# Attention inside a fused block: the products for the row maxima ahead of the weighing in TensorE's order

## The reference, cut to what matters

```python
qkv = x @ W_qkv                      # 16 heads of 64
q, k = apply_rope(q), apply_rope(k)
dots = jnp.einsum('bhid,bhjd->bhij', q, k) * scale
dots = jnp.where(causal, neg, dots)
attn = jax.nn.softmax(dots, axis=-1)
out = jnp.einsum('bhij,bhjd->bhid', attn, v)
out = jax.nn.relu(out @ W_o1) @ W_o2
```

## Time and profile before

| | us |
|---|---|
| median of three runs (5065.14 to 5069.31) | 5067.33 |
| the profiled execution | 5057.61 |
| its span, first to last instruction | 5056.0 |
| VectorE busy | 3705.1 (73%) |
| TensorE busy (matmuls) | 3693.8 (73%) |
| ScalarE busy | 2569.0 (51%) |
| POOL busy | 2388.5 (47%) |
| largest group: L2242, `low_part`, 640 times | 783.7 |
| next: L2269, `maximum`, 748 times | 667.0 |

### The profile page before, as it was taken

The page is one execution under the profiler, slowest core; times in us unless marked ns, Lnnn a source line. Parts: engine busy times, 40 slices in busy tenths (PEclk is TensorE's granted clock), DMA queues, the critical chain, the costliest instruction groups (busy, mean ns, idle before and its releaser), DMA issues. The chain is left out here.

```text
span 5056.0 us, 84627 instructions
## 1 busy us (share of the span) xinstructions
PE 3693.8 (73%) x28905; PEld 2609.3 (52%) x28907; DVE 3705.1 (73%) x4463; ACT 2569.0 (51%) x4134; POOL 2388.5 (47%) x1532
## 2 busy tenths in 40 slices
PE   2997645555555569948936898989989899894595
PEld 1663224444444446637813566666656566663484
DVE  6883489999999988840067888888888888885101
ACT  1222456666666632222313677777767676684221
POOL 0220268888888842221034665655656666600202
PEclk9998777777676779959957999999999999996697
DMA  2000001000000100024532222222222222202255
GB/s 86 0 0 4 7 21 32 30 29 29 29 31 30 30 29 0 0 91 146 175 113 58 57 51 52 48 47 68 53 64 54 50 54 52 55 10 92 73 182 155
DMA packets 236313, 276.22 MB, mean 55 GB/s; under 512 B 63820, under 2 KB 183557, under 8 KB 234561
## 3 DMA queue, kind: packets, MB, share of 16 engines
q1 hardware_dynamic: 223056, 244.85, 17.7%
q0 software_dynamic: 8704, 24.35, 1.4%
q10 hardware_dynamic: 4224, 2.76, 0.3%
HBM read 152.60 MB, written 36.04 MB: 37 GB/s over the span
## 5 line engine op out<-in xcount | busy, mean ns | idle before, releaser
L2242 DVE TENSOR_TENSOR att_b_prob_low<-att_b_prob,att_b_prob_high 128x1024 f16<-128x1024 f32 (+2 forms) x640 | 783.7, 1225 | 54.5 <-ACT att_b_prob_high L2209 49.0
L2269 DVE TENSOR_REDUCE att_b_neg_max<-att_b_peek 128x1 f32<-128x1024 f32 (+1 forms) x748 | 667.0, 905 | 143.3 <-PE att_b_peek L2097 114.0
L2207 ACT ACTIVATE att_b_prob<-att_b_score,att_soft 128x1024 f32<-128x1024 f32 (+2 forms) x640 | 633.0, 989 | 223.7 <-PE att_b_score L2120 148.0
L1025 PE MATMUL mix_scan_hT<-ident,mix_scan_h 128*128 128x128 f32 x1024 | 253.3, 395 | 526.6 <-DVE mix_scan_h L973 498.6
L2209 ACT ACTIVATE att_b_prob_high<-att_b_score,att_soft 128x1024 f16<-128x1024 f32 (+2 forms) x640 | 630.1, 985 | 10.2 <-PE att_b_o L2148 3.5
L1025 PEld LDWEIGHTS mix_scan_hT<-ident,mix_scan_h 128*128 128x128 f32 x1024 | 176.5, 200 | 640.7 <-DVE mix_scan_h L973 445.1
L2144 PE MATMUL att_b_o<-att_b_vh,att_b_prob_high 128*128 128x65 f16 x4352 | 463.1, 195 | 37.2 <-DVE att_b_prob_low L2242 26.5
L2118 PE MATMUL att_b_score<-att_b_q_both,att_b_k_twice 128*128 128x512 f16 (+3 forms) x1280 | 448.9, 351 | 28.6 <-ACT att_b_prob_high L2209 18.3
L2144 PEld LDWEIGHTS att_b_o<-att_b_vh,att_b_prob_high 128*128 128x128 f16 x4352 | 401.4, 98 | 130.4 <-DVE att_b_prob_low L2242 71.5
L2148 PE MATMUL att_b_o<-att_b_vh,att_b_prob_low 128*128 128x65 f16 x4352 | 461.8, 194 | 0.0
L2146 PE MATMUL att_b_o<-att_b_vl,att_b_prob_high 128*128 128x64 f16 x4352 | 461.4, 193 | 0.0
(11 more groups left out here) (343 smaller groups left out, 9606.0 us busy)
## 6 DMA issues: line engine op xcount, KB each, us to landing
moe_w<-in_L_ffn_W_dram SPq DMA_DIRECT2D x64, 1024.0 KB, 8.2
mix_scan_b_row<-mix_b_rows SPq DMA_DIRECT2D x128, 256.0 KB, 3.1
att_b_crossed<-att_b_raw SPq DMA_DIRECT2D x512, 64.0 KB, 2.0
att_b_q_both<-att_b_halves SPq DMA_DIRECT2D x240, 64.0 KB, 2.0
att_b_k_twice<-att_b_halves SPq DMA_DIRECT2D x240, 64.0 KB, 2.0
moe_slots_in<-moe_route_zero SPq DMA_DIRECT2D x2, 4096.0 KB, 14.3
moe_exp_x<-moe_slots_in SPq DMA_DIRECT2D x32, 256.0 KB, 4.5
moe_slots_out<-moe_exp_y POOLq DMA_DIRECT2D x32, 256.0 KB, 6.4
```

What stands on the lines that cost most here:

```text
L1025: last = pe.transpose(hT_ps[:, j * D + m * P:j * D + (m + 1) * P], hs[:, b * W + m * GRP + t * P:b * W + m * GRP + (t + 1) * P], ident[:, :])
L2207: act.activation(prob[:, at:at + width], score[m % 2][:, 0:width], ACT.Exp, scale=soft[:, 0:1])
L2242: dve.tensor_tensor(prob_low[:, at:at + width], prob[:, at:at + width], prob_high[:, at:at + width], ALU.subtract).then_inc(low_ready, 1)
L2269: last = dve.tensor_reduce(neg_max[:, first + col:first + col + 1], peek_bank(kind, s)[:, base:base + nb * P], AX.X, ALU.max, negate=True)
```

## The change

In TensorE's order within a step `peek` stands in front of `weigh` instead of behind it. The orders of the other engines and all semaphore counts are as before, and so are all operations.

```diff
                     if has_piece(kind, v):
                         scores(t, b, v, kind)
-                    if v >= 2 and has_piece(kind, v - 2) or v < 2 and has_piece(kind, -1):
-                        weigh(t, b, v - 2)
                     peek_at = slot_at(kind, v)
                     if peek_at:
                         peek(t, b, kind, *peek_at)
+                    if v >= 2 and has_piece(kind, v - 2) or v < 2 and has_piece(kind, -1):
+                        weigh(t, b, v - 2)
                     job = side_job(kind, v)
                     if job:
                         side(t, b, *job)
```

## The result

The kernel got **0.8% slower**: 5105.29 us median of four runs (5102.17 to 5109.34) against 5066.24 (5061.6 to 5069.31) of the kernel before, ratio 1.0082, 95% interval 1.0071 to 1.0094. That is +39 us where +55 was forecast, inside the range and with the forecast's sign. The profiled execution took 5102.17 us, its span 5100.6: 44.6 us more than the profiled execution before, whose time lay 9.7 us under its median of three.

What follows compares the result with a forecast made beforehand. Attention keeps VectorE 86% and TensorE 89% busy; POOL sets steps 1 to 21, later steps lack cover. Terms 2.66 + 0.63 + 0.39 = 3.68 us a pair, times 15, give 55 us slower: 5122 us, range 5062 to 5187.

Steps and rivals of the forecast that it cites:

- the last pair: The pair of heads with no successor to prepare; the forecast multiplied its loss by the 15 other pairs only.
- Steps 23 to 39: Second part of a pair, without cover from POOL: late maxima delay TensorE, 2.66 us a pair.
- the four terms: Late maxima at steps 24, 26, 28, 34: 1.36, 1.61, 0.59, 1.43 us, less 2.33 us of waits already there.
- a wait taken at the latest step serves its neighbours: Steps 23 to 39: TensorE then stands later against VectorE, so only the peaks of lateness were counted.
- Step 22: The weighing, formerly ahead of the wait for keys, now runs behind it with all that follows: 0.63 us a pair.
- Step 0: Late maximum delays the next pair's first projection, so POOL's unbroken run starts later: 0.39 us a pair.
- Steps 1 to 21: Costed at nothing: small losses end in a shorter wait for keys, 5.41 us, at step 22.
- Set by POOL: Steps 1 to 21: POOL's rotations run without a break until the keys step 22 needs, and set the time.
- Faster: Rival: early products feed a starving VectorE; at most 54 us of the maxima's idle time goes, 5013 us; chance 0.12.
- no change: Rival: TensorE takes its waits at other places and VectorE loses 6 us, 5073 us, within 0.2%; chance 0.12.
- The ring: Rival: maximum, products, weighing, exponential, subtraction release each other, 4.92 us per two steps, nearly everywhere; 5187 us; chance 0.12.
- The clock: Rival: more waits bring more falls of TensorE's clock, 6 us on top of the forecast, 5128 us; chance 0.04.

Runs made afterwards that it cites:

- the first two experiments: New order only in steps 23 to 39, then only in steps 0 to 22, against the kernel before: ratios 1.0081 and 1.0002.
- the fourth experiment: Changed kernel with the old order again at steps 24, 26, 28 and 34: 5104.43 us, ratio 1.0050 to the kernel before.
- short maxima: Each row maximum over half its columns: 5079.98 us (1.0024) with the new order, 5015.08 us (0.9900) with the old, ratios to the kernel before.
- the fifth experiment: Changed kernel with four halves of `prob_high` in place of two: 5116.12 us, ratio 1.0103 to the kernel before.
- M first: New order only in steps 23 to 39, with VectorE's maximum ahead of the low-half subtraction from step 24: 5116.35 us, 1.0083 to the kernel before.
- the kernel with both edits: Kernel before with the new order in steps 1 to 21 and step 22's products for the maxima behind the values job: 5041.89 us, 0.9943.
- The two gains: Against the kernel before: new order only in steps 0 to 21, 0.9967; old order with step 22's products behind the values job, 0.9968.

## Why the prediction was right, and where it was not

The number came out in part by luck: the mechanism of the largest term held, one term was sized too high, and two places put at nothing, the run on POOL and the last pair, erred in opposite directions.

**Steps 23 to 39: 2.66 us predicted, 2.98 measured.** The mechanism, K behind a late M with W and the scores queued behind it, is shown by the first two experiments and by K's idle time (28.5 to 152.6 us). The sizes of the four terms were good in sum (2.63), off by up to 0.37 us singly (step 34, 1.09 in place of 0.72), and step 30's 0.50 us was not among them. L in pieces 21 to 38 took 21.36 us a pair before and 21.03 after, so none of it is longer work on VectorE: it is waiting. That a wait taken at the latest step serves its neighbours fits the sum but isn't shown by it; the fourth experiment shows the other side: spare the four, and two thirds of the loss are met elsewhere.

**Step 22: 0.63 us predicted, 0.64 measured** (3.33 to 3.97 us from K to the scores). What the prediction did not see is that the place is worth more than that to whoever keeps it free: 1.15 us for W, and, with the values job moved as well, 3.33 - 0.62 = 2.71 us there, of which steps 23 to 39 (45.34 to 46.53) take back 1.19.

**Step 0: 0.39 us predicted, 0.18 measured.** POOL's run started 8.60 us after the turn in place of 8.42.

**Steps 1 to 21: nothing predicted, 1.32 us gained.** This is the step that failed: 20 us over the 15 pairs. The other terms, larger by 0.18 us a pair together, took 3 us of it back and the last pair 5, so that the forecast was 11 us too high by the profiled executions and 16 by the medians. The sum of the first part is 0.18 for the later start, -1.32 for a shorter run on POOL, 0.06 for the DMAs behind it, 0.64 at step 22: -0.44 us. "Set by POOL" was right, and it was wrong to take POOL's run as fixed, and so to expect at best a shorter wait from steps 1 to 21. Two of its five lines in the groups of before:

```profile
L1869 POOL TENSOR_TENSOR att_b_crossed<-att_b_crossed,att_b_sin 128x512 f32<-128x512 f32 x120 | 195.6, 1630 | 0.0
...
L1874 POOL TENSOR_TENSOR att_b_halves<-att_b_raw,att_b_halves 128x512 f16<-128x512 f32 x120 | 176.4, 1470 | 10.0
```

and of after:

```profile
L1869 POOL TENSOR_TENSOR att_b_crossed<-att_b_crossed,att_b_sin 128x512 f32<-128x512 f32 x120 | 226.2, 1885 | 0.0
...
L1874 POOL TENSOR_TENSOR att_b_halves<-att_b_raw,att_b_halves 128x512 f16<-128x512 f32 x120 | 154.2, 1285 | 10.0
```

The same operations, the same shapes: one line got 30.6 us longer, the others together 50.9 us shorter (987.1 us for the five before, 966.8 after), which is 20.3 us over all eight rotations of the 15 pairs. In the six of the run the operations got 1.92 us a pair shorter (51.07 to 49.15), and 0.58 us of it went into new idle time between them: the run is no longer unbroken. L on VectorE, over pieces 0 to 20 of a pair, went the other way, 27.55 to 30.04 us, and this is where VectorE's longer busy time is. The timeline of the changed kernel shows the trade:

```profile
3340.29 1.21 DVE L2242 TENSOR_TENSOR att_b_prob_low<-att_b_prob,att_b_prob_high 128x1024 f16<-128x1024 f32 x1
3340.32 2.31 POOL L1869 TENSOR_TENSOR att_b_crossed<-att_b_crossed,att_b_sin 128x512 f32<-128x512 f32 x1
...
3342.71 1.27 POOL L1870 TENSOR_TENSOR att_b_raw<-att_b_raw,att_b_crossed 128x512 f32<-128x512 f32 x1
...
3342.83 2.22 DVE L2242 TENSOR_TENSOR att_b_prob_low<-att_b_prob,att_b_prob_high 128x1024 f16<-128x1024 f32 x1 [0.59 <-ACT att_b_prob_high L2209]
```

Whichever starts second is longer by about what is left of the first: L started first (3340.29) and took its 1.21 us, POOL's operation took 2.31 in place of 1.27; 2.4 us later POOL was first, and L took 2.22 in place of 1.21. The Trainium skill (SBUF — State Buffer, SBUF: two separate sides) says just this: VectorE, reading two operands from SBUF, and GpSimd take a shared pair of ports as an exclusive lock, and the one that comes second is fully blocked; the rows agree, 1.04 and 1.01 us. One pairing in this trace does not agree: L started 68 times inside POOL's L1873, which reads one operand, with 0.72 us of it left on the mean, and was 0.02 us longer on the mean. Over all pairs L comes second hardly more often than before (334 times in place of 328), but with 0.62 us left of POOL's operation in place of 0.51, and POOL's operations behind L with 0.73 left in place of 0.79. Against the times that both take undisturbed (here the lowest tenth of each kind), L lost 135 us by it in place of 107, and POOL 193 in place of 215. That is most of L's 31.8 us and all of POOL's 20.3. POOL's run is what steps 1 to 21 wait for, and L there is not, so this trade is a gain. It belongs to the phase and not to the order: with short maxima it is the old order that has the short run (51.51 us) and the new one the long (53.18).

**The rivals.** "Faster" lost, though its premise held: M's idle time fell by 80.6 us, more than the 54 that were priced. What fed VectorE sooner in the second half took from the work behind K. Here the trace decides against the Trainium skill (Perfetto Trace Analysis, Optimization Strategy) as the prediction applied it: the dependence that ended VectorE's gaps did start sooner, and the time rose. TensorE, which the change made wait, was as full in this stretch as VectorE (89% and 86%). Of "no change" the part on the first half was near the truth (ratio 1.0002 for all but the second half), though by a shorter run on POOL, which it did not name: the waits of K in those steps and the later W at step 22 are in that kernel, and are paid for. The ring fell with the fifth experiment, for steps 23 to 39 at least. The clock did not swing more: it was granted at 0.97 and 0.98 in the stretch, with 124 us more of waits on M.

**The last pair: nothing predicted, 5.1 us lost.** It has K in its steps 0 to 15 and no keys to wait for at step 22, so nothing covers it; the sum counted the 15 pairs with a successor alone. The kernels with the old order in steps 1 to 21 and whole maxima took 83.97 to 84.52 us for it, those with the new one and two halves of `prob_high` 89.21 to 90.91, and the one with the new order and four halves 85.86. So here, other than in steps 23 to 39, the exponential behind W makes up most of the loss.

**What stays open.** In the second half the loss could not be split between the handshake over the one buffer and VectorE's load: opening the ring (48.27), shorter maxima (2.05 us left) and M first (47.75) each take away a part at most. A second buffer for K, which would test the handshake by itself, was not tried.

## What to carry to other kernels

In an in-order queue an instruction that may wait belongs behind all that is ready and that others wait for; how late its releaser is, step by step, against the moment at which it would reach the queue's head gave the price within about a tenth here (2.66 against 2.98 us), though not step by step. Count the turns that lack the cover, too, such as the last one. Where there is a long wait, put as much ready work as there is in front of it: done there it shortened the wait here, and behind it it ran mostly at the 1.2 GHz level. A stretch that is set by another engine is not of a fixed length: before counting it at nothing, look at whether that engine's operations have two durations in the trace, and at what runs beside the longer ones.

## What the runs showed that was not expected

- POOL's run of six rotations took 51.5 to 53.3 us for identical work, by phase against L for the most part, and moves worth 20 us came from that.
- The work behind the wait at step 22 ran at granted clocks of 0.57 and 0.59 after noted waits of 3.53 and 5.41 us, and at 1.00 after one of 2.70 us. In the kernel with the new order up to step 21 only, K to the scores took 1.77 or 1.78 us in six pairs of twelve, against 3.09 to 3.39 us in every pair of the kernel before. A short noted wait is no promise, though: in the kernel with both edits K(22) came after one of 2.01 us, and K(23) took 1.03 us, at a granted clock of 0.50.
- The two gains, 0.33% and 0.32%, came to 0.57% together.
